# Two grouped attentions of a decoder: value products in pairs, output products two units behind, square roots later

## What is computed

```
# B: cross attention, keys and values from the context, rotary positions, mask from the input
q = query @ Wq          # 32 heads of 128
k, v = ctx @ Wk, ctx @ Wv   # 8 heads of 128, each shared by a group of 4 query heads
q = q * cos + rotate_half(q) * sin ; k the same
attn = softmax(where(mask == 0, -1e9, q k^T / sqrt(128)))
x = (attn @ v) @ Wo
# D: self attention of the same shapes, causal mask, no rotation
```

## Time and profile before

| what | before |
|---|---|
| median of 3 runs | 1681.94 us |
| profiled execution: own time / span of its instructions | 1676.39 us / 1674.6 us |
| PE busy | 1581.4 us (94%) |
| PEld busy | 1267.2 us (76%) |
| DVE busy | 984.5 us (59%) |
| ACT busy | 660.6 us (39%) |
| granted TensorE clock, mean | 0.988 |

### The profile page before, as it was taken

One profiled execution on the slowest core, in us unless ns is written; L12 is line 12 of the kernel. 1 busy time (PEld: TensorE's weight loads), 2 busy tenths in 40 slices (PEclk: granted clock), 3 DMA queues, 4 the chain that ended last, 5 costly groups with the idle time before them and its releaser, 6 DMA issues. The chain is left out here.

```text
span 1674.6 us, 22788 instructions
## 1 busy us (share of the span) xinstructions
PE 1581.4 (94%) x8504; PEld 1267.2 (76%) x8504; DVE 984.5 (59%) x1958; ACT 660.6 (39%) x1209; POOL 201.2 (12%) x146
## 2 busy tenths in 40 slices
PE   8788799999999999999889999999999999889998
PEld 6566587787788778876777788788878877676876
DVE  5998767766765776677433542552453346246755
ACT  4476434433433443333333332332332322436541
POOL 8321040000000000000340000000000000613330
PEclk9899999999999999999999999999999999999999
DMA  6111011101110110100111110110110000202231
GB/s 227 33 33 45 13 51 51 64 14 39 38 51 1 64 51 13 39 13 26 45 52 39 38 51 1 62 50 13 50 50 25 27 25 25 68 20 81 78 85 50
DMA packets 26023, 75.44 MB, mean 45 GB/s; under 512 B 3888, under 2 KB 4624, under 8 KB 25680
## 3 DMA queue, kind: packets, MB, share of 16 engines
q1 hardware_dynamic: 25552, 73.16, 13.2%
q0 software_dynamic: 384, 1.05, 0.2%
HBM read 72.10 MB, written 2.10 MB: 44 GB/s over the span
## 5 line engine op out<-in xcount | busy, mean ns | idle before, releaser
L83 PE MATMUL bankY<-sb_Dwo,sb_DoT 128*128 128x512 f32 x768 | 194.0, 402 | 0.3 <-DVE sb_DoT L1082 0.3
L83 PE MATMUL bankY<-sb_Bwo,sb_BoT 128*128 128x512 f32 x768 | 192.1, 399 | 0.2 <-DVE sb_BoT L1082 0.2
L83 PE MATMUL bankA<-sb_xT,sb_Bwq 128*128 128x512 f32 x768 | 190.5, 397 | 0.5 <-issue 0.5
L83 PE MATMUL bankA<-sb_xT,sb_Dwq 128*128 128x512 f32 x768 | 189.9, 396 | 0.0
L83 PEld LDWEIGHTS bankY<-sb_Dwo,sb_DoT 128*128 128x128 f32 x768 | 141.0, 189 | 42.3 <-issue 13.3
L83 PEld LDWEIGHTS bankY<-sb_Bwo,sb_BoT 128*128 128x128 f32 x768 | 139.9, 188 | 41.6 <-issue 12.9
L83 PEld LDWEIGHTS bankA<-sb_xT,sb_Bwq 128*128 128x128 f32 x768 | 142.3, 188 | 34.8 <-issue 3.6
L83 PEld LDWEIGHTS bankA<-sb_xT,sb_Dwq 128*128 128x128 f32 x768 | 142.2, 188 | 33.9 <-issue 2.7
L1013 DVE TENSOR_TENSOR sb_BqT<-bankA,sb_Btable 128x512 f32<-128x512 f32 x64 | 44.3, 692 | 150.1 <-ACT sb_Bsw L910 150.1
L1049 DVE TENSOR_TENSOR sb_xtok<-sb_xtok,bankY 128x512 f32<-128x512 f32 x128 | 87.2, 681 | 53.0 <-PE bankY L83 52.9
L910 ACT ACTIVATE sb_Bsw<-bankA 64x512 f32<-64x512 f32 x160 | 94.8, 593 | 54.8 <-PE bankA L83 51.7
(11 more groups left out here) (277 smaller groups left out, 2969.5 us busy)
## 6 DMA issues: line engine op xcount, KB each, us to landing
sb_raw<-in_w_attn SPq DMA_DIRECT2D x80, 512.0 KB, 3.5
sb_raw<-in_q_gu SPq DMA_DIRECT2D x22, 256.0 KB, 2.7
sb_raw<-in_q_d SPq DMA_DIRECT2D x11, 256.0 KB, 2.6
sb_raw<-in_wqk SPq DMA_DIRECT2D x8, 256.0 KB, 2.6
sb_rawx<-in_xT SPq DMA_DIRECT2D x4, 512.0 KB, 6.4
sb_raw<-in_ctxT SPq DMA_DIRECT2D x4, 512.0 KB, 6.3
sb_xtok<-in_x_tok SPq DMA_DIRECT2D x1, 2048.0 KB, 13.2
sb_raw<-in_ctx_tok SPq DMA_DIRECT2D x4, 512.0 KB, 3.8
```

Of the source, the lines that this page charges most:

```text
L83: last = nc.tensor.matmul(out, lhs, rhs, start=start and i == 0, stop=stop and i == len(pairs) - 1)
```

## The change

oT becomes one tile per part with room for two units; unit v has side v % 2 of it, and side v % 2 of both banks of bankO. Which value products run in slot u is said by `attended`: none in an even slot and those of u - 1 and u in an odd one, but one by one in slots 6, 7, 14, 15 of B and in slots 14, 15 of D's last group (`alone`). ACT's and DVE's copies out of bankO are one instruction for a pair. Output product u - 2 now stands in slot u, ahead of the value products; slots 7 and 15 have three. ACT's exp stands ahead of its copy out of bankO. DVE's residual is that of unit u - 3. The square root of the first four tiles moves on ACT from the end of slot 14 to behind slot 15's copy.

```diff
-            oT = [[sb(mem, f"{tag}oT{i}{p}", [P, GROUP, 2, S], F32R) for p in range(2)] for i in range(2)]
+            oT = [sb(mem, f"{tag}oT{p}", [P, 2, GROUP, 2, S], F32R) for p in range(2)]
...
+            def alone(u, final):
+                return u % NT >= NT - 2 and (rope or (final and u >= NT))
+
+            def attended(u, last):
+                return (u,) if alone(u, last) else (u - 1, u) if u % 2 else ()
...
+                    def attend(part, u):
+                        units = attended(u, part.final)
+                        if units and u < NT:
+                            pe.wait_ge(v_done, part.it * 4 + u // 2 + 1)
+                        for v in units:
+                            if v == units[0]:
+                                pe.wait_ge(pt_done, part.unit(u) + 3)
+                                pe.wait_ge(o_low, part.unit(v) + 1)
+                            for b in range(2):
+                                rows = slice(S * b, S * b + S)
+                                done = nc.tensor.matmul(bankO[:, b, side(v)], V[rows, v % NT, v // NT * HD:(v // NT + 1) * HD], pt[v % 2][rows, :], start=True, stop=True)
+                            done.then_inc(o_ready, 1)
...
-                            if late(u):
-                                output(part, u - 1)
...
-                            if u % NT and not late(u):
+                            if u % NT >= 2:
+                                output(part, u - 2)
+                            attend(part, u)
+                            if u % NT == NT - 1 and alone(u, part.final):
                                 output(part, u - 1)
...
                             if u % NT == NT - 1:
+                                if not alone(u, part.final):
+                                    output(part, u - 1)
                                 output(part, u)
...
-                            act.wait_ge(o_ready, part.unit(u) + 1)
-                            nc.scalar.activation(oT[u % 2][0][:].rearrange("p h b q -> p b h q"),
-                                                 bankO[:, :, 0:GROUP * S].rearrange("p b (h q) -> p b h q", h=GROUP), ACT.Copy).then_inc(o_high, 1)
                             if not late(u) and (u + 2 < SLOTS or not part.final):
                                 exp(part, u + 2)
+                            units = attended(u, part.final)
+                            if units:
+                                act.wait_ge(o_ready, part.unit(u) + 1)
+                            if len(units) == 1:
+                                nc.scalar.activation(of_unit(0, u), unit_bank(u), ACT.Copy).then_inc(o_high, 1)
+                            elif units:
+                                nc.scalar.activation(of_pair(0), pair_bank, ACT.Copy).then_inc(o_high, 2)
+                            if part.final and u == SLOTS - 1:
+                                ln_roots(act, norm + 1, 0)
...
-                            if part.final and u == SLOTS - 2:
-                                ln_roots(act, norm + 1, 0)
...
-                            if u % NT >= 2:
-                                residual(part, u - 2)
-                            dve.wait_ge(o_high, part.unit(u) + 1)
+                            if u % NT >= 3:
+                                residual(part, u - 3)
+                            units = attended(u, part.final)
+                            if units:
+                                dve.wait_ge(o_high, part.unit(u) + 1)
...
+                            elif units:
+                                nc.vector.tensor_tensor(of_pair(1), pair_bank, f32(of_pair(0)), ALU.subtract).then_inc(o_low, 2)
...
                             if u % NT == NT - 1:
+                                residual(part, u - 2)
                                 residual(part, u - 1)
```

More of the change, by code:

```diff
@@ L721, in grouped_attention, with side, of_pair, of_unit @@
                 dst[f"o{i}"] = dst[f"o{i + 2}"] = o
+            def side(v):
+                return slice(v % 2 * GROUP * S, (v % 2 + 1) * GROUP * S)
+            def of_pair(i):
+                return oT[i][:].rearrange("p v h b q -> p b (v h) q")
+            def of_unit(i, v):
+                return oT[i][:, v % 2].rearrange("p h b q -> p b h q")
+            pair_bank = bankO[:].rearrange("p b (h q) -> p b h q", q=S)
+            unit_bank = lambda v: bankO[:, :, side(v)].rearrange("p b (h q) -> p b h q", q=S)
+            def alone(u, final):
+                return u % NT >= NT - 2 and (rope or (final and u >= NT))
+            def attended(u, last):
+                return (u,) if alone(u, last) else (u - 1, u) if u % 2 else ()
             def run(engine, start, turn):
@@ L834, in output @@
                         pe.wait_ge(y_done, part.unit(u) + 1)
-                        pairs = [x for h in range(GROUP) for x in three([o[:, h].rearrange("p b q -> p (b q)") for o in oT[u % 2]], [w[:, h, :] for w in wo])]
+                        pairs = [x for h in range(GROUP) for x in three([o[:, u % 2, h].rearrange("p b q -> p (b q)") for o in oT], [w[:, h, :] for w in wo])]
                         if u % NT == NT - 1:
@@ L1078, in turn @@
                                      back(part, u + 1) if u + 1 < SLOTS or not part.final else None)
-                            if u % NT >= 2:
-                                residual(part, u - 2)
-                            dve.wait_ge(o_high, part.unit(u) + 1)
-                            nc.vector.tensor_tensor(oT[u % 2][1][:].rearrange("p h b q -> p b h q"), bankO[:, :, 0:GROUP * S].rearrange("p b (h q) -> p b h q", h=GROUP),
-                                                    f32(oT[u % 2][0][:]).rearrange("p h b q -> p b h q"), ALU.subtract).then_inc(o_low, 1)
+                            if u % NT >= 3:
[3 more added lines that the diff above has]
+                                dve.wait_ge(o_high, part.unit(u) + 1)
+                            if len(units) == 1:
+                                nc.vector.tensor_tensor(of_unit(1, u), unit_bank(u), f32(of_unit(0, u)), ALU.subtract).then_inc(o_low, 1)
+                            elif units:
+                                nc.vector.tensor_tensor(of_pair(1), pair_bank, f32(of_pair(0)), ALU.subtract).then_inc(o_low, 2)
                             if u % NT == 0:
```

## The result

| what | before | after |
|---|---|---|
| median (lowest to highest), runs | 1681.59 us (1680.12 to 1682.49), 4 | 1711.31 us (1711.15 to 1717.01), 4 |
| ratio, 95% interval | | 1.0184 (1.0164 to 1.0203) |
| profiled execution: own time / span | 1676.39 / 1674.6 us | 1711.15 / 1709.3 us |
| granted TensorE clock, mean | 0.988 | 0.980 |

Slower by 29.7 us, where 29 was forecast. The page's totals first: PE is as busy as before (1580.8 against 1581.4 us). What grew is the time in which it is not.

The account below looks back on a forecast made before the run. PE's instruction stream was taken as the bound in B and D. B's other halves 31.5, last halves +3 and -8.2 + 0.5 in D, norms 2.4 sum to +29 us: 1711 us, range 1690 to 1725.

Parts of the forecast that it names:

- both waits: PE in B: about 2.3 us for oT at slots 2 and 10, about 2.0 us for bankY at 7 and 15.
- Saving on PE: Value products in B and D: a second unit behind the first saves 0.40 us, 55 pairs, 22 us.
- Slots 0 to 2 and 8 to 10 of B: Late oT makes output 8 wait 2.3 us; +2.6 us in a second half, +2.4 in a first.
- Slot 7 and 15: In B, output 6 waits 2.0 us for bankY, held until unit 4's residual at +6.64 us.
- D: Attention D: pairs save, output 0 and 8 wait 0.4 us; -1.2 us a half, -8.2 us over 7 halves.
- Last half of B and the norms: Waits of 1.4 and 2.3 us in slots 12 and 14; +3 in B's last half, +1.2 in each norm.
- The unknown sizes: Pair's copy and subtraction out of two banks: lower sizes 1.04 and 1.23 us taken; upper would add 5 us in all.
- number 1: Rival: ACT's copy is not really held behind exp, so output waits 1.0 us in B; 1699 us, chance 0.10.
- number 2: Rival: only the waits for oT come, bankY is free in time; 14 us less, 1697 us, chance 0.08.
- number 3: Rival: faster, the queues keep up with the output two slots later; 1658 us, chance 0.09.
- 4: Rival: partly hidden, half of the waits vanish later; between 1676 and 1690 us, chance 0.08.
- 5: Rival: worse, drain stays for each unit or copies cost more, waits chain through slots 3 to 6; 1718 to 1735, chance 0.13.

Follow-up runs that it names:

- experiment three: Changed kernel with bankY given back ahead of the rotation in slots 7 and 15 and the copy out of bankO ahead of exp: 1682.69 us.
- the last experiment: Changed kernel with B and D's last half in the old order and the copy out of bankO ahead of exp everywhere: 1667.53 us.

## Why the prediction was right

The forecast came true, 1711.31 us against 1711, and the mechanism with it: both waits stand where they were put, at nearly the size that was given. That the total is right within 1 us is luck, since an error of about 5 us and one of about 6.5 us met (the last point). By step:

- **Saving on PE.** 0.40 us a pair was said; D's group gives 0.41. The 8 products do run as one block, 1.06 us against 1.07. That the price is that of the way in and out of the other tiling is argued, not shown.
- **Slots 0 to 2 and 8 to 10 of B.** oT was put at +8.25 after T(9), and the output product starts at 492.88 - 484.62 = +8.26. The wait is 1.96 where 2.3 was said, because the profile counts it from the modelled end of the transposes, 0.44 us after their start, and I counted from 0.15 after it. The new wait of unit 9's transposes is 0.36 for 0.55. A first half of the middle groups came to +3.9 us (65.5 against 61.6) for +4.4, a second half, less its half-clock stretch, to about +4.4 for +4.6.
- **Slot 7 and 15.** The residual of unit 4 was put at +6.64 after T(7) and ends at 471.69 - 465.05 = +6.64. The wait is 2.14 for 2.0, and worth 15.3 us by the slots of experiment three for 14.
- **D.** -9.5 us for -7.7. A half gives -1.4 and not -1.2 (seven halves at -1.2 are -8.4, and not the -8.2 of the sum), and its last half about +0.1 for +0.5.
- **Last half of B and the norms.** Waits of 1.25 and 2.15 us in slots 12 and 14 for 1.4 and 2.3. The last half came to +2.9 (48.9 against 46.0) for +3, but a stretch of 1.0 to 1.6 us is in it, which the sum did not have. So the waits and savings alone come to +1.3 to +1.9. The root's load lengthened the way from value product 15 to the residual of unit 15 from 6.41 to 7.34 us, +0.9 for +1.2.
- **The unknown sizes.** The pair's copy takes 1.01 to 1.03 us and its subtraction 1.23 (1225 ns in the group's row above): the lower bound, which I took.
- **What the sum did not have.** The half-clock stretches: 5 in B, two in slot 10 at 1.0 us, one each in slots 7 and 15 at 1.6, and one in slot 14 of the last group, which no row shows without a stretch; about 6.5 us. Without them the rows of the two traces give 31.2 + 1.1 - 9.5 + 1.4 = 24.2 us, against 29. So the steps were sized about 5 us too dear (some 2 us in B's halves ahead of the last, over 1 in its last half, 1.8 in D), and the clock was left out. Without the stretches the median would have lain near 1705, inside the range too.

Of the rivals, number 1 (the copy not held) is refuted by the chain of exp, copy and subtraction above; number 2 (bankY free in time) by 15.0 us of waits; number 3 (faster) by both; 4 and 5 by the time, and 5's drain for each unit by the 0.42 us of a second unit. None of them had that a wait also has a price on the clock, which is why two mended waits were worth more than their sum.

## What to carry to other kernels

Grouping these products saved 0.41 us a pair, and it moved a longer copy behind whatever stood next in each queue. Before grouping, follow the result through every engine to its consumer, in the stage where those engines are least idle. The same edit lost 37 us in the stage with 30% of DVE free and won 9 in the one with over half of it free, so choose such an order stage by stage, and put the copy that PE waits for ahead of work with slack. Where a buffer is returned later, look for the place at which the queue returns it, not for the average load.

## What the runs showed of the hardware that was not expected

- **Half clock after waits of some 2 us.** In a stream in which PE was otherwise busy, 35 of 59 waits of 1.96 to 2.21 us had a stretch of 3 to 3.5 us at granted clock 0.50 behind them, each costing 1.0 us in slots 2 and 10 and 1.6 in slots 7 and 15. None of the waits in B of 1.57 us or less (7 of 1.46 to 1.57 in the run with B one by one) had. Waits between 1.57 and 1.96 us did not occur. Why one wait of 2 us is followed by it and the next is not stays open, since I made no run that sets the length of a wait alone.
- **The mean clock differs between executions of one kernel, and the time with it.** The five runs of the last experiment gave 0.988, 0.985, 0.983, 0.981 and 0.982 at 1663.35, 1665.85, 1667.53, 1669.74 and 1670.20 us. A single profiled execution can thus lie 5 us beside the median, as the one of before did.
- **"Issue" in a profile can be a missed releaser.** 15.7 us of wait were filed as waiting for nothing. In the one shown, DVE's subtraction had ended 0.10 us earlier, and the total fell to 5.9 us when the copy that feeds it was moved.
